# Late count scatters of a four-layer graph network: started in unify, one stage later

## What is computed

```
edge_index = [src, dst]
x = x + L0(x)                        # two graph attentions (4 and 8 heads), ELU, product with Wu, residual
x = x + L1(relu(layernorm(x)))       # five rounds of message passing: segment_sum(norm * (h[src] + edge_fea), dst)
x = x + L2(relu(layernorm(x)))       # mean over h[col], with x @ W + b
x = x + L3(relu(layernorm(x)))       # edge MLP, segment_sum over rows, GRU
```

## Time and profile before

| | |
|---|---|
| median of 3 runs | 3934.1 us (3929.52 to 3937.01) |
| profiled execution: time, span | 3943.29 us, 3941.3 us |
| mean granted TensorE clock | 0.922 |
| busy: PE, DVE, POOL, ACT | 3238.0, 2285.6, 2122.0, 1314.1 us |
| scatters of the loop (L1020) | 352, 1.70 us each |
| late scatters (L343) | 32, 8 in the attention stage, 24 in unify |

### The profile page before, as it was taken

The page is one execution under the profiler, slowest core; times in us unless marked ns, Lnnn a source line. Parts: engine busy times, 40 slices in busy tenths (PEclk is TensorE's granted clock), DMA queues, the critical chain, the costliest instruction groups (busy, mean ns, idle before and its releaser), DMA issues. The chain is left out here.

```text
span 3941.3 us, 67198 instructions
## 1 busy us (share of the span) xinstructions
PE 3238.0 (82%) x17467; PEld 2185.9 (55%) x17468; DVE 2285.6 (58%) x7121; ACT 1314.1 (33%) x3037; POOL 2122.0 (54%) x1867
## 2 busy tenths in 40 slices
PE   6277888888888788846989898989879788888978
PEld 4145666566656565534656464646444566666644
DVE  8856777778777677748222222222252566766768
ACT  0122333333333333313313131313155555555522
POOL 0356888788888888833464545452000066766710
PEclk9988999989888989868999999999989899999989
DMA  6259666566555556632553535352249244444420
GB/s 259 50 134 310 145 154 151 144 151 156 135 136 138 136 133 141 136 27 38 170 181 113 184 114 178 114 182 89 78 122 264 84 126 124 127 122 124 125 53 22
DMA packets 471410, 528.90 MB, mean 134 GB/s; under 512 B 191947, under 2 KB 376489, under 8 KB 471223
## 3 DMA queue, kind: packets, MB, share of 16 engines
q0 software_dynamic: 141664, 236.21, 24.5%
q1 hardware_dynamic: 316938, 271.68, 23.8%
q10 hardware_dynamic: 12749, 20.33, 1.4%
HBM read 437.02 MB, written 70.53 MB: 129 GB/s over the span
## 5 line engine op out<-in xcount | busy, mean ns | idle before, releaser
L1096 PE MATMUL p_out<-rows,hot 128*128 128x266 f32 x2048 | 639.2, 439 | 60.1 <-DVE rows L1233 60.0
L1020 POOL DMA_INDIRECT count_dram<-number,place x352 | 598.4, 1700 | 145.1 <-issue 109.2
L1666 POOL DMA_INDIRECT rec_dram<-records,edge_place x416 | 405.3, 974 | 436.5 <-PE p_hi L1699 223.3
L1012 POOL DMA_INDIRECT rows<-att_dram,idx x512 | 542.9, 1060 | 165.1 <-issue 120.5
L1596 PE MATMUL p_hi<-cbuf,parts 128*128 128x400 f16 x1750 | 581.9, 332 | 0.0
L1595 PE MATMUL p_lo<-cbuf,parts 128*128 128x400 f16 x1750 | 581.8, 332 | 0.0
L2176 POOL DMA_INDIRECT col_rows<-col_dram,m_idx x440 | 416.2, 946 | 250.6 <-issue 135.5
L1096 PEld LDWEIGHTS p_out<-rows,hot 128*128 128x128 f32 x2048 | 391.0, 212 | 161.1 <-DVE rows L1233 109.9
L1623 DVE TENSOR_TENSOR node_sum<-p_hi,low_sb 128x400 f32<-128x400 f32 x80 | 45.9, 574 | 572.6 <-ACT low_sb L1614 572.6
L1104 PE MATMUL p_out<-mask,ident_bf 128*128 128x240 bf16 x1788 | 360.9, 287 | 2.8 <-issue 2.8
L1233 DVE TENSOR_TENSOR rows<-rows 128x512 f32<-128x512 f32 x512 | 349.4, 683 | 0.2 <-ACT rows L981 0.2
(11 more groups left out here) (399 smaller groups left out, 6272.3 us busy)
## 6 DMA issues: line engine op xcount, KB each, us to landing
cbuf<-count_dram SPq DMA_DIRECT2D x40, 2500.0 KB, 10.2
dl_rep<-dl_dram SPq DMA_DIRECT2D x128, 256.0 KB
count_dram<-zeros SPq DMA_DIRECT2D x20, 1000.0 KB, 21.0
g_rows<-count_dram SPq DMA_DIRECT2D x25, 800.0 KB, 4.6
rec_dram<-blank ACTq DMA_DIRECT2D x1, 17600.0 KB, 74.1
m_group_rows<-rec_dram SPq DMA_DIRECT2D x110, 160.0 KB, 2.3
records<-in_edges POOLq DMA_DIRECT2D x32, 520.0 KB, 5.2
key_rep<-key_dram SPq DMA_DIRECT2D x64, 256.0 KB
```

What stands on the lines that cost most here:

```text
L1012: nc.gpsimd.indirect_dma_start(rows[r][:, u, :], None, att_dram, bass.IndirectOffsetOnAxis(ap=idx[r][:, u:u + 1].bitcast(U32), axis=0)).th ...
L1020: nc.gpsimd.indirect_dma_start(count_dram, bass.IndirectOffsetOnAxis(ap=place[r][:, n, c:c + 1].bitcast(U32), axis=0), number[r][:, 2 * n ...
L1096: m = nc.tensor.matmul(p_out[q][:, side, 0:HALF], hot[k][:, u, :], rows[k][:, u, side * HALF:(side + 1) * HALF], start=(u == 0), stop=(u = ...
L1666: nc.gpsimd.indirect_dma_start(rec_dram, bass.IndirectOffsetOnAxis(ap=edge_place[:, at:at + 1].bitcast(U32), axis=0), records[b % 3][:, j, ...
```

## The change

1. `LATE_ROUNDS` goes from 16 to 18: bodies 16 and 17 keep their second pair of group 2 back as well. `LATE_ATT` is gone; no late pair is issued in the attention stage. Unify issues pairs 0 to 13 (`LATE_UNI` = 14), the norm block 14 and 15 (`LATE_NORM` = 16), the turning block 16 and 17.
2. Trash cells lie 32 cells (64 bytes) apart, KD + 32p and KD + 4096 + 32p; there are 8192 of them.
3. SP's store of `dinv` goes from the start of unify to the start of the tables stage, ahead of the 25 stores.

```diff
-LATE_ROUNDS, LATE_ATT, LATE_UNI, LATE_NORM = 16, 4, 16, 16
+LATE_ROUNDS, LATE_UNI, LATE_NORM = 18, 14, 16
...
+APART = 32
+TRASH = 2 * APART * P
...
-                    o.did(TS(own_place[:, 0:1], pidx[:], float(KD), None, ALU.add))
-                    o.did(TS(own_place[:, 1:2], pidx[:], float(KD + P), None, ALU.add))
+                    o.did(TS(own_place[:, 0:1], pidx[:], float(APART), float(KD), ALU.mult, ALU.add))
+                    o.did(TS(own_place[:, 1:2], pidx[:], float(APART), float(KD + APART * P), ALU.mult, ALU.add))
...
                 def _(sp):
+                    sp.dma_start(dinv_dram.rearrange("(t p) -> p t", p=P), dinv[:]).then_inc(dinv_out, 16)
                     for t in range(NT):
...
                         rounds_in_two(pool, work)
-                        scatter_late(pool, 0, LATE_ATT)
                         pool.wait_ge(blank_out, 16)
...
                     def _(sp):
-                        sp.dma_start(dinv_dram.rearrange("(t p) -> p t", p=P), dinv[:]).then_inc(dinv_out, 16)
                         sp.dma_start(w2[:], a["m_W2"].rearrange("(k p) d -> p k d", k=2)).then_inc(fold_in, 16)
...
                     def _(pool):
-                        scatter_late(pool, LATE_ATT, LATE_UNI)
+                        scatter_late(pool, 0, LATE_UNI)
```

More of the change, by code:

```diff
@@ L57 @@
 PADSRC, PADDST = NP - 1, 4095
-TRASH = 1024
+APART = 32
+TRASH = 2 * APART * P
 EJ = EP // P
```

## The result

| | before | the change |
|---|---|---|
| median | 3934.1 us (3929.52 to 3944.35, 5 runs) | 3908.1 us (3901.09 to 3910.64, 5 runs) |
| ratio | | 0.9926, 95% interval 0.9908 to 0.9945 |
| profiled span | 3941.3 us | 3898.8 us |

The change is faster by 26 us by the medians, and the forecast was 3907.8 us. A ratio here is taken over all runs of both kernels, so it isn't quite that of the two medians (0.9934). In a later group on another chip the change gave 3903.81 us beside 3939.5, a ratio of 0.9912 (0.9897 to 0.9927). The two profiled spans lie 42.5 us apart, since the execution shown of before is 9 us over its median and that of after 7 us under its own. So the medians say how much, and the stages say where. What follows goes by stage.

A forecast was written before the change was run, and what follows sets the result against it. POOL was taken to bound the attention loop and DVE unify. The terms -8.6 - 37.2 + 0 + 0 + 14.5 + 5 gave -26.3 us, so 3934.1 became 3907.8 us, with a range of 3891 to 3922.

The forecast's parts named there:

- Two more late pairs: Attention loop: bodies 16 and 17 issue 10 scatters, not 12, each saving 4.3 us; -8.6 us, bounds -4 to -9.
- The end of the attention stage: Without late pairs there, unify starts 6.0 us after POOL's last loop issue, at 1708.3 instead of 1745.48: -37.2 us.
- Trash cells: Cells 64 bytes apart let the last loop scatter land before unify starts, but by itself take nothing out: 0 us.
- Unify: With 14 pairs and no store ahead, POOL needs 91.3 us against 94.1, so pairs stay hidden: 0 us, bounds 0 to +3.
- The store: Inverse roots stored in the tables stage hold POOL's first pair, with no slack at the stage's end: +14.5 us, bounds 0 to 18.
- The norm block: Two pairs in a 12.3 us block, with a wait nearer 4.5 us between them: +5 us, bounds 0 to +9.
- The turning block: Two pairs in the 16.6 us block that turns h; POOL needs 15.4 us, hidden: 0 us, bounds 0 to +3.
- B: Tables stage: the store hides, or POOL has slack at the end; -40.8 us in all, 3893 us; chance 0.15.
- C: Spacing doesn't cure the last loop scatter: +7.2 us, 3915; 14 more if the attention block's end waits for it; chance 0.12.
- D: Tables stage: the store piles up table stores and ten pairs each wait 2 us more, +20: 3928 us; chance 0.07.
- E: Norm block: the pair waits behind SP's ten loads of 4-byte pieces, 35.2 us more: slower, 3943 us; chance 0.04.

The follow-up runs named there:

- x2: The change, but with trash cells 2 bytes apart again: 3925.7 us, ratio 0.9956.
- x4: The kernel before, with only the trash cells set 64 bytes apart: 3928.09 us, ratio 0.9962.
- x1: The change, but with the store of the inverse roots back at the start of unify: 3915.76 us, ratio 0.9928.
- x8: The kernel before, with its trash cells 16 bytes apart: 3923.18 us, ratio 0.9965.
- x12: The change itself, measured once more in a later group on another chip: 3903.81 us, ratio 0.9912.
- x5: The kernel before, with only the store of the inverse roots moved to the tables stage, on the second chip: ratio 1.0054.
- x7: The change, with the wait for the blank store at the end of the attention program moved from POOL to SP: 3911.43 us, ratio 0.9924.
- x9: The change with 16 late pairs, but late tables allocated for 18 so later tiles keep the change's addresses, on the second chip: ratio 0.9934.
- x3: The change with 16 late pairs instead of 18: 3926.26 us, ratio 0.9957.
- x11: The change, with inverse roots turned by TensorE and stored as 25 rows of 512 bytes, and the long addition cut into 25: 3885.4 us, ratio 0.9866.
- x10: The change, with inverse roots stored as 25 rows of 512 bytes and the long addition cut into 25, on the second chip: ratio 0.9911.
- x6: The change, with inverse roots turned by TensorE and stored as 25 rows of 512 bytes, on the second chip: ratio 0.9927.

## Why the prediction was right, and where it wasn't

**Two more late pairs, -8.6 us.** Bodies 16 and 17 gave 5.5 in the first trace and 6.5 over all traces outside the second chip, on which it was 1.4. Outside it the bound was read rightly (POOL; bodies of 10 scatters are shorter at once); on it POOL isn't the bound of these bodies. The size was two body means subtracted, and those means hold bodies 2 to 16 and 17 to 29, which differ in more than the scatters.

**The end of the attention stage, -37.2 us.** Measured -36.4. Six us after the last issue came out as 6.73.

**Trash cells, 0 us.** Right as a term of the sum, but not for the reason given. The text said that without the spacing "the first pair of unify waits for the same landing", which would be worth 7.2 us; x2 shows 14 us, because the end of the block waits for it already. The term of -37.2 us needed the spacing. x4 shows the other half: on the kernel before, the spacing alone is worth 15 us, about half of what the whole change gives.

**Unify, 0 us.** Right: 94.3 us. The forecast that the fold loads "may use" the slack did not come true, as the second pair waits only 2.22 us beside them.

**The store, +14.5 us.** The place and the cause were right, "no slack" was not. The idle time became 14.55 us, 12.3 more than a wait of 2.2. In the first profile the stage grew by 11.7; over all traces, whatever the chip, it takes 86.0 us with the small writes in it (seven traces, 82.5 to 88.3) and 73.8 without (before, x1, x4, x8: 70.8 to 75.1), +12.2. Both numbers hold the other thing that was missed: a scatter stretched to between 4.4 and 8 us at the end of this stage. In the trace of before it was not to be seen, as its last scatter was issued until 250.72 and had begun at 249.17, just ahead of DVE's addition at 249.49. The step "with 6 us behind its last issue POOL is there at 256.7 already" used a figure of another stage's end; here the next stage starts 3.4 to 3.7 us behind POOL's last issue. So POOL would have allowed 254.3 where DVE allowed 257.56: 3.3 us of slack. The three together give the stage: 12.3 of wait + 2.9 of the stretched scatter - 3.3 of slack = 11.9.

**The norm block, +5 us.** Measured +2.6, and +2.8 in x12. The wait between its pairs was 5.39 us, more than the 4.5 assumed, but only 1.9 us follow the last issue, not 6. Two errors in opposite directions.

**The turning block, 0 us.** Right; POOL's last issue ends 4.4 us before the block does (6.8 in x12).

**What no term held:** bodies 0 and 1, -6 us, from the addresses of tiles.

By the stages of its first trace the change is worth 11.7 - 6.7 - 5.5 - 36.4 + 0.2 + 2.6 = -34.1 us (left out is what doesn't repeat between traces), where the prediction's sum was -26.3 and the medians say -26 in one group and -36 in the other (3903.81 against 3939.5). The near hit of 3907.8 on 3908.1 is partly luck, then: a store 2.8 us cheaper, a norm block 2.4 cheaper and 6.7 us in bodies 0 and 1, less the 3 us that bodies 16 and 17 gave too little in that trace, put the sum 8 us lower. The interval of the first ratio (22 to 36 us) holds all three. The range of 3891 to 3922 took in both.

**The rivals.** B, the store hides: no, a wait of 14.55 us. The rule of the Trainium skill (DMA: Bandwidth & Descriptors, Queues, rings and completion order) that DMA engines take their queues in turn did not let the pair pass; the other rule of that section, on completion counts, fits the wait, but no run tells it from a queue that is simply full. C: the spacing cures the scatter (2.10 us). D: the later pairs waited 2.2 to 2.5 us each, as always. E: the pair in the norm block waited 5.39 us, not 35 more than a quiet one: the ten loads of 4-byte pieces hold a scatter far less than 3,200 writes of 4 bytes do.

## What to carry to other kernels

The store of 3,200 pieces of 4 bytes held the next pair of scatters for 15 to 20 us in both places where it was tried; look for a stage whose engine has that slack, or make rows of it first (TensorE's turn of 128 x 25, with the long addition cut up, gave back 14.5 us of the stage and 18 of the whole). Padding that all goes "somewhere harmless" deserves addresses that are far apart, and the end of a block pays for a slow landing even if no instruction waits for it. When a term of a sum is read from one stage's end, read it from a second one before it is used there: the 6 us of this kernel were 6.7, 5.4, 4.2, 3.5 and 1.9.

## What the runs showed of the hardware that was not expected

**A scatter under VectorE's long addition.** Ten traces have a scatter of POOL in the tables stage whose issue falls under DVE's addition of 128 x 6400 elements. It takes 4.43 (after) and 4.55 us (x12) where it begins late in the addition, and 7.04 to 8.00 (x1 to x5, x7 to x9) where it begins early; the others of that stage take 1.55. In the kernel before, the last scatter begins 0.3 us ahead of the addition and takes 1.55. In x3, timeline of DVE:

```profile
251.53 6.82 DVE L833 TENSOR_TENSOR x_sb<-x_sb,h 128x6400 f32<-128x6400 f32 x1
```

and of POOL:

```profile
251.83 7.93 POOL L333 DMA_INDIRECT count_dram<-number_pre,place_pre  x1 [2.27 <-DMA count_dram<-number_pre,place_pre]
260.07 1.55 POOL L333 DMA_INDIRECT count_dram<-number_pre,place_pre  x1 [0.30 <-issue]
```

The addition ends at 258.35 and the scatter at 259.76, 1.4 us after it; in the change the addition ends at 257.13 and the scatter at 258.56, 1.4 us again, and so in all ten. So the issue wasn't done before the addition was over. The Trainium skill (SBUF — State Buffer, SBUF: two separate sides) has a lock for this: a VectorE operation with two inputs in SBUF holds the port pair that it shares with GpSimd for the whole instruction, against a GpSimd operation that reads SBUF. The traces agree, in that no stretched scatter ends before the addition does. In x11, with the addition cut into 25 of one tile, no scatter of this stage is stretched. The stage is 68.1 us there; on the second chip x10 has 68.4 and x6, which keeps the long addition, 71.3. In x6 too no scatter is stretched, as POOL's last one began 0.2 us ahead of the addition; there the addition itself ends the stage.

**Additions of 2 bytes to neighbouring cells.** 122 of them in 256 bytes: 16.75 us of wait (before), 2.94 with a cell every 16 bytes (x8), 2.10 with one every 64 (x4).

**Small writes.** 3,200 pieces of 4 bytes hold the scatters of another queue for 14.55 to 20.08 us in all eleven traces in which a pair was issued just behind them; behind 25 rows of 512 bytes, the same 12.5 KB, issued with the pair, the wait is 2.24 to 2.35 us (x6, x10, x11).

**Addresses in SBUF.** With later tiles shifted by 64 bytes, two loop bodies are some 6 us shorter while 17.6 MB are stored beside them. A difference between kernels (x9 is the one that keeps it apart from the late pairs, in one trace on another chip than x3's), not explained.

**The clock.** Ahead of the turning block TensorE does nothing for some 15 us, and the granted clock is 0.50, which is the level of 1.2 GHz. In eleven traces (before, x1 to x6, x8, x9, x11, x12) it is 0.50 through the turning block as well (16.6 us), in x10 0.57 in the mean (16.0 us), in two (after, x7) 0.85 (14.0 us). No edit goes with that.
